# Layer 1 of a two-layer conditioned attention kernel: its small products in another order, and the output products later in the next step

## The reference

```python
xn = _ln(x, ln_w, ln_b)
q = softmax((xn @ Wq + bq).reshape(b, t, h, dh), axis=-1)
k = softmax((xn @ Wk + bk + (1.0 - src_mask) * -1000000.0).reshape(b, t, h, dh), axis=1)
v = ((xn @ Wv + bv) * src_mask).reshape(b, t, h, dh)
att = jnp.einsum('bnhd,bnhl->bhdl', k, v)
y = jnp.einsum('bnhd,bhdl->bnhl', q, att).reshape(b, t, d)
scale, shift = jnp.split((silu(emb) @ W_emb + b_emb)[:, None, :], 2, axis=2)
hh = silu(_ln(y, ln2_w, ln2_b) * (1.0 + scale) + shift) @ W_out + b_out
return x + hh
```

## Time and profile before

| | us |
|---|---|
| three runs | 1054.78, 1051.83, 1053.91 |
| median | 1053.91 |
| the profiled execution | 1052.0 |
| its span, first to last instruction | 1048.6 |
| TensorE busy, share of the span | 1022.5, 98% |
| VectorE busy | 772.7, 74% |
| ScalarE busy | 610.6, 58% |
| GpSimd busy | 588.1, 56% |
| mean granted TensorE clock | 0.997 |

### The profile page before, as it was taken

One profiled execution on the slowest core, in us unless ns is written; L12 is line 12 of the kernel. 1 busy time (PEld: TensorE's weight loads), 2 busy tenths in 40 slices (PEclk: granted clock), 3 DMA queues, 4 the chain that ended last, 5 costly groups with the idle time before them and its releaser, 6 DMA issues. The chain is left out here.

```text
span 1048.6 us, 26047 instructions
## 1 busy us (share of the span) xinstructions
PE 1022.5 (98%) x8558; PEld 890.0 (85%) x8558; DVE 772.7 (74%) x1347; ACT 610.6 (58%) x2021; POOL 588.1 (56%) x871
## 2 busy tenths in 40 slices
PE   7899999999999999999997999999999999999997
PEld 6679888988889888898886888888888888888885
DVE  6656766677666766678679787878778877778886
ACT  6358676876768766776777454434434444443353
POOL 3455456555465456554577465666556555566632
PEclk9999999999999999999999999999999999999999
DMA  9752111211212111120113211222211112112101
GB/s 302 246 184 67 39 52 43 64 55 35 60 44 65 47 40 53 55 65 34 56 51 116 81 63 50 67 67 65 65 65 56 39 55 65 55 55 65 45 31 50
DMA packets 46117, 73.72 MB, mean 70 GB/s; under 512 B 8274, under 2 KB 14546, under 8 KB 46068
## 3 DMA queue, kind: packets, MB, share of 16 engines
q1 hardware_dynamic: 46066, 73.11, 21.8%
q10 hardware_dynamic: 2, 0.00, 0.0%
HBM read 56.28 MB, written 16.81 MB: 70 GB/s over the span
## 5 line engine op out<-in xcount | busy, mean ns | idle before, releaser
L683 ACT ACTIVATE prob<-prob,neg_max 128x128 f32<-128x128 f32 x512 | 198.6, 395 | 77.7 <-DVE neg_max L983 77.7
L483 POOL TENSOR_SCALAR stat<-stat 128x1 f32<-128x1 f32 x128 | 34.7, 271 | 321.7 <-DVE stat L945 295.3
L1363 PE MATMUL bank<-xt_hi,w_hi 128*128 128x256 f32 x752 | 213.8, 284 | 0.0
L1364 PE MATMUL bank<-xt_lo,w_hi 128*128 128x256 f32 x752 | 209.4, 279 | 0.0
L1365 PE MATMUL bank<-xt_hi,w_lo 128*128 128x256 f32 x752 | 209.4, 278 | 0.0
L1363 PE MATMUL bank<-w_hi,xt_hi 128*128 128x512 f32 x384 | 157.6, 410 | 0.0
L1365 PE MATMUL bank<-w_hi,xt_lo 128*128 128x512 f32 x384 | 151.2, 394 | 0.0
L1364 PE MATMUL bank<-w_lo,xt_hi 128*128 128x512 f32 x384 | 150.4, 392 | 0.0
L1364 PEld LDWEIGHTS bank<-xt_lo,w_hi 128*128 128x128 f32 x752 | 141.9, 189 | 1.3
L1363 PEld LDWEIGHTS bank<-xt_hi,w_hi 128*128 128x128 f32 x752 | 141.6, 188 | 1.5 <-DVE z_a L1027 0.2
L1365 PEld LDWEIGHTS bank<-xt_hi,w_lo 128*128 128x128 f32 x752 | 141.7, 188 | 0.0
(11 more groups left out here) (130 smaller groups left out, 2347.4 us busy)
## 6 DMA issues: line engine op xcount, KB each, us to landing
x_in<-in_x_dram SPq DMA_DIRECT2D x32, 256.0 KB, 2.7
x_res<-in_x_dram SPq DMA_DIRECT2D x32, 256.0 KB, 2.6
between_layers<-x_res SPq DMA_DIRECT2D x32, 256.0 KB, 2.0
x_in<-between_layers SPq DMA_DIRECT2D x32, 256.0 KB, 3.3
x_res<-between_layers SPq DMA_DIRECT2D x28, 256.0 KB, 2.6
out_dram<-x_res SPq DMA_DIRECT2D x28, 256.0 KB, 2.0
room<-in_L_cond_W_emb_dram SPq DMA_DIRECT2D x8, 512.0 KB, 6.6
prob<-in_L_cond_emb_w_dram SPq DMA_DIRECT2D x4, 512.0 KB, 11.2
```

The lines of the kernel that those rows point to most:

```text
L483: pool.tensor_scalar(v[:, 8:9], v[:, 7:8], EPS, None, ALU.add).then_inc(s[a_in].sem, 1)
L683: last = act.activation(prob[:, b, i, :], prob[:, b, i, :], ACT.Exp, bias=neg_max[:, b, i:i + 1], accum_out=row_sum[:, b, h:h + 1])
L1363: pe.matmul(o, a_hi, b_hi, start=start, stop=False)
L1364: pe.matmul(o, a_hi, b_lo, start=False, stop=False)
```

## The change

**TensorE.** In a step of layer 1 the small products of both sequences stand next to each other. Before, the order was (numbers are b): turn_k 0, turn_q 0, turn_k 1, output 0, keys 0, turn_q 1, keys_values 0, output 1, keys 1, query 0, keys_values 1, values 0, query 1, queries 0, turn_yn 0, values 1, queries 1, turn_yn 1, turn 0, turn 1. Now it is: turn_k 0, turn_k 1, turn_q 0, keys 0, keys 1, turn_q 1, keys_values 0, keys_values 1, output 0, output 1, query 0, query 1, values 0, values 1, queries 0, queries 1, turn 0, turn 1, turn_yn 0, turn_yn 1. (The outputs are those of the pair before.)

**GpSimd** masks the second v ahead of the two residuals instead of behind them. SyncE's program is the same. Banks are given out anew, and `drain` is reordered in the same way. The mixed step keeps its banks through a parameter. The diff, with the mixed step and parts of `drain` left out:

```diff
@@ -166,14 +166,13 @@
 
         bank = [ctx.enter_context(nc.psum_tensor(f"bank{i}", [P, D], F32)) for i in range(8)]
         FIRST = dict(X=(5, 4), PT=(4, 5), Q=(6, 7), K=(0, 1), V=(3, 6), PV=(7, 7), Y=(2, 2), H=(6, 7), O=(5, 6))
-        SECOND = dict(X=(0, 1), K=(6, 7), V=(0, 6), Q=(2, 4), KT=(2, 4), QT=(3, 3), KV=(4, 4), Y=(5, 1), H=(3, 7), O=(5, 1))
+        SECOND = dict(X=(0, 1), K=(6, 0), V=(6, 0), Q=(2, 4), KT=(2, 4), QT=(5, 5), KV=(4, 2), Y=(5, 4), H=(3, 7), O=(1, 3))
 
         MIXED = FIRST | dict(X=(0, 1), K=(6, 7), V=(0, 1), Q=(3, 4))
         BEGIN = FIRST | dict(X=(0, 1), V=(3, 4))
 
-        LATE = dict(O=(5, 5))
         LATER = SECOND | dict(H=(5, 1), O=(1, 2))
-        DRAIN = SECOND | dict(V=(0, 3), Q=(2, 4), KT=(6, 7), QT=(2, 4), KV=(0, 3), Y=(6, 7), H=(0, 3), O=(5, 4))
+        DRAIN = SECOND | dict(V=(7, 6), Q=(2, 3), KT=(0, 4), QT=(2, 2), KV=(6, 7), Y=(0, 4), H=(6, 7), O=(5, 3))
 
         LAST_OUT = dict(O=(None, 1))
 
...
@@ -600,11 +599,11 @@
     norm2(k, 0)
     v_mask(f, slot, 0)
     norm2(k, 1)
+    v_mask(f, slot, 1)
     if i == G:
         pool.wait_ge(out_in, 16)
     residual(1, k, 0)
     residual(1, k, 1)
-    v_mask(f, slot, 1)
 
 def drain(k, f):
     norm2(k, 0)
...
@@ -833,10 +832,17 @@
     tanh(k, 1)
 
 def step1(i, n, f, k, late, slot):
+    if i != G:
+        film1(late + (-1), 0)
+        tanh(late + (-1), 0)
     kt_out(k, 0)
+    kt_out(k, 1)
     qt_out(k, 0)
-    kt_out(k, 1)
     q_exps(k, 1 - slot, 1)
+    if i != G:
+        s_high(late + (-1), 0)
+        film1(late + (-1), 1)
+        tanh(late + (-1), 1)
     s_high(late + (-1), 1)
     qt_out(k, 1)
     k_exps(f, slot, 0)
...
@@ -844,20 +850,20 @@
     if i == G:
         high_part(1, WO)
         act.wait_ge(film_dve, 6)
-    film1(k, 0)
-    tanh(k, 0)
     q_exps(f, slot, 0)
-    s_high(k, 0)
-    film1(k, 1)
     xt_high(n, 1 - slot, 0, SECOND)
     xt_high(n, 1 - slot, 1, SECOND)
-    tanh(k, 1)
 
 def drain(k, f):
+    film1(k + (-GROUP), 0)
+    tanh(k + (-GROUP), 0)
     kt_out(k, 0)
+    kt_out(k, 1)
     qt_out(k, 0)
-    kt_out(k, 1)
     q_exps(k, 0, 1)
+    s_high(k + (-GROUP), 0)
+    film1(k + (-GROUP), 1)
+    tanh(k + (-GROUP), 1)
     s_high(k + (-GROUP), 1)
     qt_out(k, 1)
     k_exps(f, 1, 0)
...
@@ -1232,54 +1238,64 @@
     q_soft(f, slot, 1)
 
 def step1(i, n, f, k, late, slot):
+    q_sums(k, 1 - slot, 0)
+    if i != G:
+        silu(late + (-1), 0)
+    stats1(n, 0)
+    if i != G:
+        s_low_part(late + (-1), 0)
+    stats1(n, 1)
+    q_sums(k, 1 - slot, 1)
+    k_masked(f, slot, 0)
+    if i != G:
+        silu(late + (-1), 1)
+    k_highest(f, slot, 0)
+    k_masked(f, slot, 1)
+    s_low_part(late + (-1), 1)
     if i == G:
-        s_low_part(late + (-1), 1)
         dve.wait_ge(zeroed, 1)
-    else:
+    kv_out(k, 1 - slot, 0)
+    kv_out(k, 1 - slot, 1)
+    k_highest(f, slot, 1)
+    if i != G:
         output(SECOND, late + (-1), 0)
-    stats1(n, 0)
-    q_sums(k, 1 - slot, 0)
-    q_sums(k, 1 - slot, 1)
-    kv_out(k, 1 - slot, 0)
-    k_soft(f, slot, 0)
-    stats1(n, 1)
     output(LAST_OUT if i == G else SECOND, late + (-1), 1)
-    k_soft(f, slot, 1)
     y_norm(1, k, 1 - slot, 0)
-    kv_out(k, 1 - slot, 1)
+    k_inverse(f, slot)
     v_add(1, SECOND, f, slot, 0)
     y_norm(1, k, 1 - slot, 1)
-    k_inverse(f, slot)
+    v_add(1, SECOND, f, slot, 1)
     if i == G:
         low_part(1, WO)
     q_add(SECOND, f, 0)
     q_soft(f, slot, 0)
-    silu(k, 0)
-    v_add(1, SECOND, f, slot, 1)
-    s_low_part(k, 0)
     q_add(SECOND, f, 1)
     xt_low(n, 1 - slot, 0, SECOND)
     xt_low(n, 1 - slot, 1, SECOND)
     q_soft(f, slot, 1)
-    silu(k, 1)
-    s_low_part(k, 1)
 
 def drain(k, f):
     q_sums(k, 0, 0)
+    silu(k + (-GROUP), 0)
+    s_low_part(k + (-GROUP), 0)
     q_sums(k, 0, 1)
-    output(LATE, k + (-GROUP), 0)
-    k_soft(f, 1, 0)
+    k_masked(f, 1, 0)
+    silu(k + (-GROUP), 1)
+    k_highest(f, 1, 0)
+    k_masked(f, 1, 1)
+    s_low_part(k + (-GROUP), 1)
     kv_out(k, 0, 0)
-    k_soft(f, 1, 1)
+    kv_out(k, 0, 1)
+    k_highest(f, 1, 1)
+    output(SECOND, k + (-GROUP), 0)
     y_norm(1, k, 0, 0)
-    kv_out(k, 0, 1)
     v_add(1, DRAIN, f, 1, 0)
     y_norm(1, k, 0, 1)
     k_inverse(f, 1)
     q_add(DRAIN, f, 0)
     q_soft(f, 1, 0)
+    v_add(1, DRAIN, f, 1, 1)
     silu(k, 0)
-    v_add(1, DRAIN, f, 1, 1)
     s_low_part(k, 0)
     q_sums(f, 1, 0)
     q_add(DRAIN, f, 1)
...
@@ -1625,48 +1641,47 @@
 
 def step1(i, n, f, k, late, slot):
     turn_k(k, 1 - slot, 0)
+    turn_k(k, 1 - slot, 1)
     turn_q(k, 1 - slot, 0)
-    turn_k(k, 1 - slot, 1)
-    if i == G + 1:
-        need(1, WO)
-    if i != G:
-        output(1, SECOND, late + (-1), 0)
     keys(1, f, slot, 0)
+    keys(1, f, slot, 1)
     turn_q(k, 1 - slot, 1)
     keys_values(k, 1 - slot, 0)
+    keys_values(k, 1 - slot, 1)
     if i == G:
         output(0, LAST_OUT, late + (-1), 1)
     else:
+        if i == G + 1:
+            need(1, WO)
+        output(1, SECOND, late + (-1), 0)
         output(1, SECOND, late + (-1), 1)
-    keys(1, f, slot, 1)
     query(k, 0)
-    keys_values(k, 1 - slot, 1)
+    query(k, 1)
     values(1, SECOND, f, slot, 0)
-    query(k, 1)
+    values(1, SECOND, f, slot, 1)
     queries1(SECOND, f, slot, 0)
-    turn_yn(1, k, 0)
-    values(1, SECOND, f, slot, 1)
     queries1(SECOND, f, slot, 1)
-    turn_yn(1, k, 1)
     turn(n, 0, SECOND)
     turn(n, 1, SECOND)
+    turn_yn(1, k, 0)
+    turn_yn(1, k, 1)
 
 def drain(k, f):
     turn_k(k, 0, 0)
+    turn_k(k, 0, 1)
     turn_q(k, 0, 0)
-    turn_k(k, 0, 1)
-    output(1, LATE, k + (-GROUP), 0)
     keys(1, f, 1, 0)
+    keys(1, f, 1, 1)
     turn_q(k, 0, 1)
     keys_values(k, 0, 0)
-    keys(1, f, 1, 1)
+    keys_values(k, 0, 1)
+    output(1, SECOND, k + (-GROUP), 0)
     query(k, 0)
-    keys_values(k, 0, 1)
+    query(k, 1)
     values(1, DRAIN, f, 1, 0)
-    query(k, 1)
     queries1(DRAIN, f, 1, 0)
+    values(1, DRAIN, f, 1, 1)
     turn_yn(1, k, 0, LATER)
-    values(1, DRAIN, f, 1, 1)
     turn_k(f, 1, 0, DRAIN)
     turn_k(f, 1, 1, DRAIN)
     turn_yn(1, k, 1, LATER)
```

More of the change, by code:

```diff
@@ L1047, in output, with k_masked @@
                                   ).then_inc(s["o_out"].sem, 1)
-            def k_masked(f, slot, pair):
+            def k_masked(f, slot, pair, bk=SECOND):
                 if pair == 0:
@@ L1054, in k_masked @@
                 dve.wait_ge(*done(s["qk_pe"], f + (-GROUP - 1)))
-                from_bank = bank[SECOND["K"][pair]][:].rearrange("p (c n) -> p c n", c=2)
+                from_bank = bank[bk["K"][pair]][:].rearrange("p (c n) -> p c n", c=2)
                 kv = chunks(k_exp[:, slot, :])
@@ L1199, in step_mixed @@
                 dve.wait_ge(par_in[1], PARS[1])
-                k_masked(f, slot, 0)
+                k_masked(f, slot, 0, MIXED)
                 s_low_part(late + (-1), 1)
@@ L1205, in step_mixed @@
                 softmax(k, 1, (1, 2))
-                k_masked(f, slot, 1)
+                k_masked(f, slot, 1, MIXED)
                 softmax(k, 1, (3,))
@@ L1294, in drain @@
                 y_norm(1, f, 1, 1, DRAIN, z_a)
-                output(LATE, k + (-GROUP), 1)
+                output(SECOND, k + (-GROUP), 1)
                 output(LATER, k, 0, xn)
@@ L1409, in first_queries, with keys @@
                                 last.then_inc(s[("pa_pe", "pb_pe")[pair]].sem, GROUP)
-            def keys(l, f, slot, pair):
-                project(l, f, slot, WK, pair, (FIRST, SECOND)[l]["K"][pair], ("ka_pe", "kb_pe")[pair],
+            def keys(l, f, slot, pair, bk=None):
+                project(l, f, slot, WK, pair, (bk or (FIRST, SECOND)[l])["K"][pair], ("ka_pe", "kb_pe")[pair],
                         ("ka_out", "kb_out")[pair])
@@ L1599, in step_mixed @@
                 need(1, WK)
-                keys(1, f, slot, 0)
-                keys(1, f, slot, 1)
+                keys(1, f, slot, 0, MIXED)
+                keys(1, f, slot, 1, MIXED)
                 turn_probs(k, 0, (0, 1))
@@ L1676, in drain @@
                 turn_q(f, 1, 0, DRAIN)
-                output(1, LATE, k + (-GROUP), 1)
+                output(1, SECOND, k + (-GROUP), 1)
                 turn_q(f, 1, 1, DRAIN)
```

## The result

| | before | after |
|---|---|---|
| median (22 runs each) | 1053.29 | 1056.05 |
| lowest and highest | 1049.23, 1055.26 | 1052.79, 1058.97 |
| ratio, with its 95% interval | | 1.0027 [1.0017, 1.0037] |
| span of the profiled execution | 1048.6 | 1052.1 |
| TensorE busy | 1022.5 | 1021.5 |

The change costs 2.8 us (1.8 to 3.9), a small slowdown that the runs establish. The forecast was 1053.5: 1.5 more than the one execution that it counted from, but 0.4 under the median that was known then, so that its point says no change. The time lies in the forecast's range; that the kernel becomes slower could not be read from the point.

A forecast was written before the change was run, and what follows sets the result against it. TensorE, busy 98% of the span, was taken to bound the kernel. Twelve loop steps at 29.22 instead of 29.07 gave +1.8, the ends -0.9 + 0.65: +1.5 on 1052.0, so 1053.5, range 1046 to 1059.

The forecast's parts named there:

- the sum of +1.5: Whole kernel: twelve loop steps +1.8, ends -0.9 and +0.65, added to the profiled execution of 1052.0.
- term for step 16: Unrolled step 16: output waits about 1.4 for s_low_part, merged products give most of it back; +0.15.
- TensorE's saving (0.50): Loop step: cheaper neighbours among keys_values, queries, values and turn_yn save 0.50; TensorE alone would take 28.57.
- The two collisions: Loop step: VectorE operations with two SBUF operands wait for GpSimd instructions at two places; step becomes 29.22.
- First: Second sequence's silu on VectorE falls into GpSimd's norm1 and starts 0.55 late; step 28.57 becomes 28.8.
- Second: End of step: GpSimd's second residual holds VectorE's first subtraction; VectorE's chain moves by 0.48, step 28.8 to 29.22.
- The loop's term of the sum: Twelve loop steps, each 29.22 instead of 29.07: +1.8.
- Step 17 (-1.05): Unrolled step 17: the 1.23 wait of its second turn_k for q_add goes; -1.05 with the longer chain counted.
- The drain (+0.65, bounds 0 and 2): Drain: silu 0 and the second q_add come about 1.5 late, of which the end chain keeps 0.65.
- That the subtraction wins: Rival: the first subtraction runs ahead of GpSimd's second residual; step 28.75, time 1047.9; chance 0.34.
- That silu also falls behind L514: Rival: second silu, in norm1 of the first sequence, starts at 4.8 to 5.2; +0.85 or more a step, 1063.7; chance 0.12.
- The saving that does not come: Rival: paired queries cost what they cost apart and keys_values keep the switch; step 29.5, time 1056.8; chance 0.06.

The follow-up runs named there:

- E6: Changed kernel with v_mask 1 behind GpSimd's residuals and the second statistics behind the second low part on VectorE; 1047.82 us, 0.997 of the kernel before.
- E3: Changed kernel with layer 1's output bias and norm1's scaling and shift on GpSimd cut to 8 of 512 columns; 1041.27 us, 0.990 of the kernel before.
- E2: Changed kernel with GpSimd's residual of layer 1 adding the output bias in only 8 of 512 columns; 1048.35 us, 0.996 of the kernel before.
- E1: Changed kernel with one line moved: GpSimd's second v_mask stands behind the two residuals again; 1050.45 us, 0.998 of the kernel before.
- E4: Changed kernel with step 16's low part and the drain's transposes of y and silu ordered as before; 1051.69 us, 1.000 of the kernel before.
- E8: Changed kernel with the edits of E1 and E4 together, statistics left in place; 1048.27 us, 0.997 of the kernel before.
- E5: Changed kernel with VectorE's second statistics of the next input moved behind the second sequence's low part; 1051.62 us, 1.000 of the kernel before.
- E7: Changed kernel with the edits of E1, E4 and E5 together; 1045.86 us, 0.994 of the kernel before.

## Why the prediction was right and wrong

Two steps of the prediction failed. The first is what it counted from: the sum of +1.5 was put on one execution (1052.0) that lay 1.9 under the median known then, and this turned a forecast slowdown into a point, 1053.5, that says no change; the runs gave 1053.29 before and 1056.05 after, +2.8. On that median the same sum would have been 1055.4. The second is the sum's term for step 16, +0.15 against a measured +0.99. The mechanism of the loop, which most of the prediction is about, was right. Term by term:

- **TensorE's saving (0.50): too large, 0.33.** The pairs came as forecast (1.08; 1.70 for 1.68). The sum failed at what it put at nothing. By the averages of twelve loop steps, E6 against the kernel before, the two blocks of keys cost 0.22 more (5.74 against 5.52 apart), which had no term, and turn_yn 0.08 more where 0.04 less was forecast. The big products of values and queries cost 0.26 less (forecast 0.12), the outputs 0.10 less (no term), keys_values 0.14 less (0.15), `query` 0.13 less (0.19). In the way to output 1, too, keys stood at 5.55, from an estimate by columns. TensorE of E6, then of the changed kernel, where the block took 5.53 (its start, and the start of what follows it):

```profile
793.48 0.36 PE L1379 MATMUL bank<-xt_hi,w_hi 128*128 128x256 f32 x1
...
799.22 0.60 PE L1516 MATMUL bank<-ident,room 128*128 128x128 f32 x4
```
```profile
795.59 0.36 PE L1379 MATMUL bank<-xt_hi,w_hi 128*128 128x256 f32 x1
...
801.12 0.60 PE L1516 MATMUL bank<-ident,room 128*128 128x128 f32 x4
```

  So TensorE alone needs 28.73 and not 28.57.
- **The two collisions: right in place, partners and order; too large by 0.15.** First: forecast 0.23 a step (28.57 to 28.8), measured 0.12 to 0.13 (E3 against E2 and E1). Second: forecast 0.42, measured 0.36 (E1). They stand on a base that was 0.16 too low, so the two errors cancel: 29.24 against 29.22. The loop's term of the sum was good to 0.3 us, partly by luck. The hole stands where it was forecast, in front of output 1 and released by the low part: that was ready 13.7 us after `turn` 0 in step 22 (776.63 against 762.93), as 13.2 + 0.48 says; in step 23 it was 13.35.
- **Step 16 (+0.15): the term that failed most, +0.99.** I let the merged products give back most of a wait of 1.4. They save 0.33 in a step, and not even the forecast's 0.50 would have done it. The wait for the low part was 0.97, less than the 1.4; another of 0.35, for `q_add` in front of the second turn_k, which now stands ahead of turn_q, was not in the sum. The two waits less the saving are the 0.99.
- **Step 17 (-1.05): -0.88.** The hole of 1.23 went; the late low part of step 16 left a wait of 0.4 for xt_low, which was not counted.
- **The drain (+0.65, bounds 0 and 2): +1.03.** E4 shows that the late transposes of y and the late silu cost 1.10 by themselves, E1 that the second collision adds 0.37; without both the drain gains 0.43 (51.68 in E8 against 52.11). The forecast had silu 1.5 late where it was 2.25, and the second cause not at all.
- **What it was counted from.** The terms sum to +1.5 where the traces give +3.2 in layer 1 and +0.26 ahead of it. The single executions of the kernel before lie between 1049.2 and 1055.3, and its medians were 1053.29, 1052.27 and 1051.57 in three sessions. So a single execution is not a base for a change of 1.5 us: taking it moved the point by more than the whole forecast change.
- **The rivals.** That the subtraction wins was the near one, and E1 shows that it would have given 28.88 a step rather than 28.75 and 4.5 us less in layer 1. Place and closeness were right: in the changed kernel the subtraction came about 0.24 behind the start of the second residual in one kind of step (the forecast said 0.2) and about 0.06 behind it in the other, lost in nearly all, and won in one (0.73 us at 703.73) and in every second one of E5. That silu also falls behind L514 (now L513) did not happen, but it happened to the low part in E5, E6 and E7. The saving that does not come was refuted by the pairs.

## What to carry to other kernels

When VectorE's work is moved ahead of something that TensorE waits for, write down what GpSimd does at that moment: an operation with two operands in SBUF that comes just behind the start of a GpSimd instruction waits for nearly all of it (0.69 us became 1.77), and moving one line on GpSimd was worth 4.5 us in layer 1, more than the 4.0 that TensorE saves in twelve steps. Spend the same care on the unrolled steps at both ends as on the loop: one line left in the loop's order cost 2 us in steps 16 and 17, against 2.1 for all twelve loop steps. And a saving of TensorE is real only up to the next operand; put what is not needed at once (here the statistics of the next input) behind what is. Last, put a forecast change on the median of several runs and not on the one that was profiled.

## What the runs showed of the hardware

- VectorE's operations on two SBUF operands and GpSimd's do not share their time; who starts first decides. The same subtraction takes 0.69 us undisturbed, 0.80 to 0.86 where it comes just before GpSimd's second residual starts, and 1.75 to 1.80 just behind that start (E5 and the changed kernel). A low part issued 0.08 us behind the start of a 1.30 us operation took 1.77 (E5). The Trainium skill, "SBUF — State Buffer", Who interferes with whom, says that the one that starts first holds the shared port for its whole instruction and the other is blocked. By it E5's low part would take 1.91 us, the 1.22 that were left of L513 and its own 0.69; the trace agrees to 0.14, by which the measured 1.77 is shorter.
- Matmuls of 256 columns run at two paces with the same neighbours among themselves: 48 of them take 5.73 to 5.74 us (120 ns each) in all loop steps of E3, E6 and E7, and 5.53 to 5.57 (115 to 116 ns) in nine of the twelve loop steps of the changed kernel. In these nine TensorE had paused for about 0.2 us ahead of them, and what the pause cost came back but for 0.04 us at most. A pause does not explain it alone: step 21 of the changed kernel has one of 0.2 us and 5.73, step 17 of E6 one of 0.8 and 5.73. The cause is open.
- Outside the steps compared here, TensorE waits 5.0 us in the mixed step for GpSimd's normalized y, in the kernels before and after alike, and 1.0 with less work in GpSimd's queue (E3). Whether this time can be had with all the work done was not tried.
